# A hybrid transformer block on one core: who copies queries, keys and probabilities in the local attention

## The reference, cut to what matters

```python
def _layer(x, wqkv, qs, ksc, wo, lg, lb, w1, b1, w2, b2):
    h = shift_token(x)
    q, k, v = jnp.split(h @ wqkv, 3, axis=-1)          # then split in 8 heads of 64
    q = l2norm(q) * qs
    k = l2norm(k) * ksc
    q, k = rotary_xpos(q, k)
    o = local_attention(q, k, v)                       # own window and the one before, softmax
    x = x + o.transpose(0, 2, 1, 3).reshape(b, n, INNER) @ wo
    ...                                                # layernorm, gated MLP, residual
```

## Time and profile before

| | |
|---|---|
| median of 3 runs | 3673.62 us (3668.25 to 3678.44) |
| the profiled execution | 3671.41 us, its span 3669.6 us |
| TensorE matmul busy in the span | 3249.5 us (89%) |
| VectorE, ScalarE, GpSimd busy | 2666.0, 2061.8, 1798.2 us |
| the four local-attention stages | some 325 us each, starting near 1670, 2075, 2865 and 3270 us |

### The profile page before, as it was taken

The page is one execution under the profiler, slowest core; times in us unless marked ns, Lnnn a source line. Parts: engine busy times, 40 slices in busy tenths (PEclk is TensorE's granted clock), DMA queues, the critical chain, the costliest instruction groups (busy, mean ns, idle before and its releaser), DMA issues. The chain is left out here.

```text
span 3669.6 us, 86970 instructions
## 1 busy us (share of the span) xinstructions
PE 3249.5 (89%) x32714; PEld 2440.9 (67%) x32714; DVE 2666.0 (73%) x5718; ACT 2061.8 (56%) x4823; POOL 1798.2 (49%) x1631
## 2 busy tenths in 40 slices
PE   4899999998999999798998999987987799899998
PEld 3677887787887878655665566655665466656665
DVE  5577777777777777477777677776998677767775
ACT  4566666666666666325665466623443566546662
POOL 3355555555555555235664366622222566436662
PEclk8699999999999999899999999997999899999999
DMA  4111111111111110142122211231221212221122
GB/s 128 26 26 26 26 27 26 29 26 27 31 34 26 26 26 13 35 115 56 45 68 68 65 45 48 71 92 48 73 59 42 50 45 68 63 72 45 45 73 73
DMA packets 406989, 182.42 MB, mean 50 GB/s; under 512 B 233552, under 2 KB 381744, under 8 KB 404016
## 3 DMA queue, kind: packets, MB, share of 16 engines
q1 hardware_dynamic: 406576, 176.87, 19.6%
HBM read 94.20 MB, written 40.12 MB: 37 GB/s over the span
## 5 line engine op out<-in xcount | busy, mean ns | idle before, releaser
L1205 POOL TENSOR_TENSOR delta_cv<-delta_cv,delta_last_tap 96x256 f32<-96x256 f32 (+1 forms) x384 | 332.0, 865 | 587.0 <-DVE delta_cv L1646 585.8
L1985 POOL TENSOR_TENSOR g_a_rn<-g_a_clip,held_minus_half 128x16 f32<-128x16 f32 x64 | 186.4, 2912 | 263.2 <-DVE g_a_clip L2249 263.2
L1985 POOL TENSOR_TENSOR f_a_rn<-f_a_clip,held_minus_half 128x16 f32<-128x16 f32 x64 | 186.3, 2911 | 260.9 <-DVE f_a_clip L2249 232.6
L2202 ACT ACTIVATE f_a_pr<-f_ps,f_a_nb,f_a_rn 128x128 f32<-128x128 f32 x512 | 185.9, 468 | 146.8 <-DVE f_a_nb L2283 146.8
L2202 ACT ACTIVATE g_a_pr<-g_ps,g_a_nb,g_a_rn 128x128 f32<-128x128 f32 x512 | 185.9, 468 | 146.0 <-DVE g_a_nb L2283 146.0
L1474 ACT ACTIVATE delta_cv<-delta_ps,delta_conv_qk 96x256 f32<-96x256 f32 x256 | 121.9, 476 | 231.9 <-PE delta_ps L1299 230.8
L1638 DVE SCALAR_TENSOR_TENSOR delta_cv<-delta_ps,delta_conv_qk,delta_cv 96x256 f32<-96x256 f32 x256 | 122.0, 477 | 168.6 <-ACT delta_last_tap L1476 166.5
L1243 PE MATMUL delta_ps<-delta_state,delta_qk 96*128 96x192 f32 x1024 | 197.4, 336 | 10.9 <-issue 10.2
L1638 DVE SCALAR_TENSOR_TENSOR delta_cv<-delta_ps,delta_conv_v,delta_cv 128x256 f32<-128x256 f32 x192 | 92.2, 480 | 134.4 <-ACT delta_last_tap L1476 131.5
L1243 PEld LDWEIGHTS delta_ps<-delta_state,delta_qk 96*128 96x128 f32 x1024 | 165.5, 192 | 17.8 <-issue 14.4
L1474 ACT ACTIVATE delta_cv<-delta_ps,delta_conv_v 128x256 f32<-128x256 f32 x192 | 90.9, 473 | 142.8 <-PE delta_ps L1299 141.0
(11 more groups left out here) (349 smaller groups left out, 10348.3 us busy)
## 6 DMA issues: line engine op xcount, KB each, us to landing
f_a_vm<-f_a_v SPq DMA_DIRECT2D x128, 130.0 KB, 2.3
g_a_vm<-g_a_v SPq DMA_DIRECT2D x128, 130.0 KB, 2.3
delta_gd<-delta_dram_row SPq DMA_DIRECT2D x16, 1024.0 KB, 4.8
window_vm<-window_v SPq DMA_DIRECT2D x64, 128.0 KB, 2.4
f_m_x<-y SPq DMA_DIRECT2D x24, 256.0 KB, 3.5
delta_dram_inv<-delta_sub SPq DMA_DIRECT2D x16, 256.0 KB, 2.1
f_m_more<-x SPq DMA_DIRECT2D x16, 256.0 KB, 4.0
held_table<-const_rotation SPq DMA_DIRECT2D x4, 1024.0 KB, 6.7
```

The lines of the kernel that those rows point to most:

```text
L1205: pool.tensor_tensor(cv[0:M, t % 3], cv[0:M, t % 3], last_tap[0:M, t % 3], ALU.add).then_inc(summed.sem, 1)
L1985: pool.tensor_tensor(rn[:, u % 2], clip[:, u % 2], minus_half[:], ALU.pow).then_inc(rn_sb.sem, 1)
L2202: e = act.activation(pr[:, u % 2, half, i, :], ps[:, score_bank(u, half), i * P:(i + 1) * P], ACT.Exp, bias=nb[:, u % 2, half, i:i + 1], s ...
```

## The change

ScalarE copies the queries ahead of the second squares. VectorE copies the keys, in the place where it copied the odd probabilities. ScalarE copies both halves of the probabilities. The semaphores and their counts stay as they are; each copy carries the same waits as before, on its new engine.

```diff
-        def copy_kt(u):
-            act.wait_ge(*kt_ps.upto(u))
-            s_ps.need(act, u - 2)
-            s = u % RING
-            act.activation(kt[:, :, 2 * s:2 * s + 2, :], ps[:, B6, :].rearrange("p (i b k) -> p i b k", b=2, k=W), ACT.Copy)\
-                .then_inc(kt_sb.sem, 1)
-
-        def copy_pt(u):
-            pt_ps.need(act, u, 1)
-            o_ps.need(act, u - 2, 1)
-            act.activation(pt[:, u % 2, 0], ps[:, score_bank(u, 0), :].rearrange("p (i k) -> p i k", k=P), ACT.Copy)\
-                .then_inc(pt_even.sem, 1)
+        def copy_pt(u, half):
+            pt_ps.need(act, u, half + 1)
+            o_ps.need(act, u - 2, half + 1)
+            act.activation(pt[:, u % 2, half], ps[:, score_bank(u, half), :].rearrange("p (i k) -> p i k", k=P), ACT.Copy)\
+                .then_inc((pt_even, pt_odd)[half].sem, 1)
...
             if within(u):
                 square(u, 0)
                 copy_v(u)
-                square(u, 1)
             if within(i + 1):
                 copy_qt(i + 1)
+            if within(u):
+                square(u, 1)
             if within(i):
-                copy_pt(i)
-            if within(i + 1):
-                copy_kt(i + 1)
+                copy_pt(i, 0)
+                copy_pt(i, 1)
             if within(i - 1):
                 copy_ot(i - 1)
...
     def vector(dve, after):
-        def copy_pt(u):
-            pt_ps.need(dve, u, 2)
-            o_ps.need(dve, u - 2, 2)
-            dve.tensor_copy(pt[:, u % 2, 1], ps[:, score_bank(u, 1), :].rearrange("p (i k) -> p i k", k=P)).then_inc(pt_odd.sem, 1)
+        def copy_kt(u):
+            dve.wait_ge(*kt_ps.upto(u))
+            s_ps.need(dve, u - 2)
+            s = u % RING
+            dve.tensor_copy(kt[:, :, 2 * s:2 * s + 2, :], ps[:, B6, :].rearrange("p (i b k) -> p i b k", b=2, k=W)).then_inc(kt_sb.sem, 1)
...
-            if within(i):
-                copy_pt(i)
+            if within(i + 1):
+                copy_kt(i + 1)
             if 0 < u < TILES:
                 squared_norms(dve, u)
```

## The result

| | before | after |
|---|---|---|
| median | 3676.03 us (4 runs, 3668.25 to 3681.82) | 3644.15 us (4 runs, 3637.74 to 3646.66) |
| the profiled execution | 3671.41 us, span 3669.6 | 3646.51 us, span 3644.7 |
| sum of the four stages, first to last S | 1247.1 us | 1217.0 us |

The ratio is 0.9912, with a 95% interval of 0.9888 to 0.9936: 32 us, or 0.9%, faster. Forecast was a time of 3629 us, 44 us faster; the time lies inside the range of 3611 to 3655, and three quarters of the gain came. It does not lie in the band of the forecast's own case (3614 to 3640) but in that of the rival "partly eaten" (3640 to 3656).

What follows compares the result with a forecast made beforehand. TensorE sets the pace but waits for the keys copy in ScalarE's queue. 25 periods of 0.46 us less, with edges of +0.5, give 11.0 us a stage, 44 in four: forecast 3629 us, range 3611 to 3655.

Steps and rivals of the forecast that it cites:

- the forecast's own case: Whole kernel: each ordinary period gets 0.38 to 0.54 us shorter, giving 3614 to 3640 us; 69%.
- partly eaten: Rival: GpSimd's margin, a dearer keys copy or worse steps 26 to 30 take a third of the gain; 3640 to 3656, 14%.
- The limiting chain: Ordinary step: TensorE to project_v, copy_v, transposes of ks, ScalarE's queue to the keys copy, mask matmuls; 0.46 us less a period.
- The keys copy at 0.68: VectorE, ordinary step: copying the keys from PSUM takes 0.68 us, and the mask matmuls start 0.10 after it.
- Both probabilities on ScalarE, free: ScalarE's queue: one 0.48 us slot replaces another in a queue of the same length, at no cost.
- The queries ahead: ScalarE, ordinary step: worth nothing by itself, but without it the transposes of o eat 0.15 of the 0.46 us.
- GpSimd comes 0.78 later, and the covers hold: Ordinary step: rn, rot and ks come 0.78 us later from the mask matmuls' start; margins 0.2 and 0.45 remain.
- The statistics in steps 26 and 27: Next MLP's statistics on VectorE, held until rot ends: periods change by +0.46, 0 and -0.46 us.
- The first two periods, -0.3 a stage: Start of each stage: the pipeline is filling and rot or ks is late already, so together -0.3 us.
- The last period, +0.83: End of each stage: transposes of ks wait for GpSimd, 0.78 later, and the copy is some 0.05 longer; +0.83 us.
- The slower rival: Ordinary step: rn holds nb to its end, 1.25 us, making the period 10.84 and the time about 3752 us; 6%.

Runs made afterwards that it cites:

- E3: The kernel before with only the queries copy moved ahead of the second squares: 3678.95 us, ratio 1.0012 to the kernel before.
- E2: The changed kernel with the second squares back ahead of the queries copy: 3643.09 us, ratio 0.9925 to the kernel before.
- E4: E1 with the next MLP's statistics on VectorE moved behind the normalizing of the following step: 3621.31 us, ratio 0.9875 to the kernel before.
- E6: The changed kernel with GpSimd's rot of tile 1 waiting for nb of tile 0, once a stage: 3628.84 us, ratio 0.9882 to the kernel before.
- E1: The changed kernel with the old order of copies and squares in step -1 alone: 3631.99 us, ratio 0.990 to the kernel before.
- E5: E4 with the old order of copies and squares in step 29 as well: 3626.12 us, ratio 0.9876 to the kernel before.
- E7: E5 and E6 together: 3615.70 us against 3670.39 for the kernel before, ratio 0.985.

## Why the prediction came out as it did

**The limiting chain: right, to 0.01 us.** S waits for the keys, the keys waited in ScalarE's queue. 0.46 a period was worked out, 0.453 measured over 100 periods, and E3 shows that TensorE's other wait limited nothing: its removal gave nothing.

**The keys copy at 0.68: right** (0.69). **Both probabilities on ScalarE, free: right**; they are 1.10 us for two.

**The queries ahead: half wrong.** That it is worth nothing by itself is right (E3). That the keys' gain needs it (0.15 of the 0.46) is wrong (E2): four transposes shown as 0.63 us let the next matmul start after 0.48. And it isn't free at the start: it delays the second squares of tile 1 (E3, 5 us in the first periods).

**GpSimd comes 0.78 later, and the covers hold: right,** though the first without the 0.2 that was to be left. By the waits of the stretch the weight load of the transposes of q is now released by rot in many steps (19 times from 2890 to 3150, 4.5 us in sum), and no matmul moves by it: the period is 9.60.

**The statistics in steps 26 and 27: right**, 10.75, 10.75, 9.60 as forecast, by a hold of 2.02 (forecast about 2). E4 confirms the mechanism.

**The first two periods, -0.3 a stage: the step that failed**, by 11 us of the missing 14 (-1.2 forecast, +9.7 measured). The term stood there without a row, on the ground that rot or ks is late already. That fits stage 1, where VectorE is busy with the MLP before and the sum of squares is late in any case; its first two periods did stay (21.18, 21.28). For stages 2 to 4 I never followed VectorE's queue at the new wait. There the keys of tile 0 come 3.9 us after VectorE is free, and behind copy_kt's wait stood the sum of squares. I named that in the ordinary step and not in step -1. The size then came from a second thing, which I had in the sum elsewhere: rot holds a VectorE instruction with SBUF operands. I had asked whether nb runs into rn in the ordinary step (it doesn't, 1.63 us in), and not whether it runs into rot at the start (E6). Of the added time some 4.8 us over stages 2 to 4 are the stretches at the lower clock (E6), which no term of the sum held.

**The last period, +0.83: sized too small**, at 1.4 on average. The GpSimd lateness was right: where the clock stays up it is 9.25 (stage 4 of the changed kernel, E1 in all stages), against 8.40 before. The 9.71, 9.96 and 10.14 of the changed kernel's stages 1 to 3 are the clock, which had no term in my sum: at the end of these periods it is at the lower level (0.51 from 1974.8 to 1977.0, 0.50 from 2370.8 to 2373.8 and from 3159.3 to 3162.7), and 1.00 from 3549.8 to 3559.1 in stage 4 and in the last period of E1 (2353.3 to 2362.5) and of the kernel before (2378.1 to 2386.5). TensorE waits 1.22 us for rot there in the changed kernel and in E1 alike. Over all profiles, last periods with that wait lost clock in 12 of 24 stages, those with a wait of about 0.46 (the kernel before, E3, E5, E7) in none of 16. What decides among the 24, I can't say from these runs: E6 has 9.25 in three stages and 10.24 in one. It stays open, and is worth up to 1 us a stage.

**The total: inside the range, in part by luck.** The rival "partly eaten" (14%) named GpSimd's margin, a dearer keys copy and worse steps 26 to 30. Only the last of these came, with some 2 us; most of the loss lies in a place that no case named.

**The slower rival** (nb held by rn) did not come: nb takes 0.17 at 1.63 us. Whether an earlier nb would be held was not tried. The Trainium skill (SBUF — State Buffer, SBUF: two separate sides) has the port pair locked for the whole instruction, for VectorE operations with two SBUF inputs as well. The trace agrees for rot (nb held 2.30 us, to its end; L2642, with one input in SBUF, is held 2.02 in the same way) and disagrees for rn, in which nb runs freely from 1.63 us on.

## What to carry to other kernels

Time the last thing a waiting engine waits for, and move only that: of two waits shown as 0.35 and 0.31 us, ending the later one sooner was worth 0.45 us a period and taking away the earlier one nothing. Price such a wait from start to start of the engine's work, since the shown idle time can be too short. When a wait is added to an engine in a software pipeline, walk through the first and the last steps with the same care as the middle, since there the thing waited for comes at another time, and ask what stands behind the wait in the queue. When another engine is made later by some tenths, look what now falls beside it: here an addition on GpSimd slid over a tiny VectorE product and held it for 2.3 us, and one wait of GpSimd for that product took it back.

## What the runs showed of the hardware

- A GpSimd addition of 1024 numbers a partition (2.35 us) holds a VectorE product of two SBUF operands, or a tensor_scalar from SBUF, that comes after it, until it has ended: 2.30, 2.02 and 0.52 us for work that takes 0.17 alone. GpSimd's product of 512 numbers (ks, 1.04 us) does so too (0.68 us in the kernel before). The power of 16 numbers (2.91 us) does not, from 1.63 us after its start.
- A group of four 128x128 f32 transposes is shown as 0.60 to 0.66 us at full clock, and the next matmul starts 0.44 to 0.49 us after the group does.
- A hold of 2.3 us cost 2.1 us of the period where TensorE's clock stayed at its upper level behind the wait (12.06 and 12.07 against 9.93 to 9.98), and 3.3 to 4.4 where it was at the lower level there (13.22, 13.40, 14.36).
